# Expert layers on one core: the order of a pair's second matrix product and a later pair's first

## The reference, cut to what matters

```python
# layers 1 and 3 (F = 256): every token goes to one of 8 experts
h = jax.nn.gelu(xt @ W1[e], approximate=False) @ W2[e]
out = out + gate[:, None] * h
# layers 4 and 6 (H = 512): every token goes to its two best experts
h = jax.nn.gelu(jnp.einsum('bsd,dh->bsh', x, w1) + bb1, approximate=False)
y = jnp.einsum('bsh,hd->bsd', h, w2) + bb2
```

## Time and profile before

| | us |
|---|---|
| median of three runs | 1098.59 |
| the profiled execution | 1097.48 |
| its span, first to last instruction | 1095.7 |
| TensorE matmuls (PE) busy | 649.6 (59% of the span) |
| VectorE (DVE) busy | 763.3 (70%) |
| ScalarE (ACT) busy | 524.1 (48%) |
| GpSimd (POOL) busy | 544.0 (50%) |
| mean granted TensorE clock | 0.789 of full speed |

### The profile page before, as it was taken

The page is one execution under the profiler, slowest core; times in us unless marked ns, Lnnn a source line. Parts: engine busy times, 40 slices in busy tenths (PEclk is TensorE's granted clock), DMA queues, the critical chain, the costliest instruction groups (busy, mean ns, idle before and its releaser), DMA issues.

```text
span 1095.7 us, 18289 instructions
## 1 busy us (share of the span) xinstructions
PE 649.6 (59%) x5212; PEld 508.6 (46%) x5212; DVE 763.3 (70%) x2362; ACT 524.1 (48%) x1160; POOL 544.0 (50%) x562
## 2 busy tenths in 40 slices
PE   7014752579831467254698980387884469977810
PEld 7013541268720355253587870144563348765600
DVE  7884685989988457479376774499878737654742
ACT  3611333757560033052387881377874138854800
POOL 0006656587100463651767776554312467675575
PEclk9998975689955589555699996688886569986955
DMA  9602321000020133121233341111101024323232
GB/s 302 177 0 46 86 66 47 24 4 2 2 77 0 32 76 83 45 73 39 53 85 78 90 68 46 39 35 32 34 14 45 25 54 83 79 74 63 63 108 72
DMA packets 82494, 66.27 MB, mean 60 GB/s; under 512 B 10665, under 2 KB 74026, under 8 KB 82402
## 3 DMA queue, kind: packets, MB, share of 16 engines
q0 software_dynamic: 13728, 28.02, 11.7%
q1 hardware_dynamic: 68674, 37.09, 11.6%
HBM read 38.99 MB, written 26.08 MB: 59 GB/s over the span
## 4 chain that ended last, share of the span: by engine, by line
PE 28%; DVE 11%; issue 9%; POOL 6%; ACT 5%; another core or an unknown queue 4%; DMA 1%; DVEq 0%; ACTq 0%; POOLq 0%
PE bank L770 6%; POOL rt L1300 5%; PE bank L751 4%; PE bank L771 3%; PE bank L753 3%; PE bank L752 3%; ACT turned L826 1%; PE bank L735 1%; DVE turned L1123 1%; PE bank L1846 1%; PE bank L1810 1%; DVE x L1188 1%; ACT turned L831 1%; PE bank L1778 1%
## 5 line engine op out<-in xcount | busy, mean ns | idle before, releaser
L1277 POOL DMA_INDIRECT turned<-xrows_moe,token x234 | 253.0, 1081 | 313.1 <-DVE token L1043 203.1
L1300 POOL DMA_INDIRECT rt<-y_moe,slot_i x176 | 177.0, 1006 | 132.5 <-issue 53.1
L826 ACT ACTIVATE turned<-bank,b1T 128x256 f32<-128x256 f32 (+1 forms) x372 | 131.3, 444 | 93.5 <-remote 41.8
L751 PE MATMUL bank<-rt,w1h 128*128 128x128 bf16 (+1 forms) x528 | 138.2, 265 | 53.7 <-issue 24.9
L1123 DVE TENSOR_TENSOR turned<-turned 128x1024 bf16<-128x1024 f32 (+1 forms) x119 | 127.8, 1074 | 38.6 <-ACT turned L831 23.1
L752 PE MATMUL bank<-rt,w1h 128*128 128x128 bf16 (+1 forms) x528 | 137.1, 263 | 1.8 <-issue 1.7
L753 PE MATMUL bank<-rt,w1l 128*128 128x128 bf16 (+1 forms) x528 | 136.7, 262 | 1.0 <-issue 0.7
L770 PE MATMUL bank<-w_1s,turned 128*128 x624 | 120.1, 284 | 12.1 <-DVE turned L1123 6.1
L771 PE MATMUL bank<-w_1s,turned 128*128 x624 | 114.2, 226 | 2.6 <-issue 2.6
L817 ACT ACTIVATE turned<-bank 128x512 f32<-128x512 f32 x40 | 23.9, 598 | 161.1 <-issue 86.1
L1188 DVE SCALAR_TENSOR_TENSOR x<-rt,small,x 128x128 f32<-128x128 f32 x176 | 55.9, 347 | 58.6 <-DMA rt<-y_moe,slot_i 53.2
(11 more groups left out here) (334 smaller groups left out, 1750.5 us busy)
## 6 DMA issues: line engine op xcount, KB each, us to landing
y_moe<-arena SPq DMA_DIRECT2D x119, 128.0 KB
xrows_moe<-xn SPq DMA_DIRECT2D x8, 512.0 KB
turned<-xrows_moe,token POOLq DMA_INDIRECT x234
rt<-y_moe,slot_i POOLq DMA_INDIRECT x176
x<-in_x SPq DMA_DIRECT2D x4, 512.0 KB, 5.7
arena<-in_w SPq DMA_DIRECT2D x1, 2048.0 KB, 9.6
xn<-in_w SPq DMA_DIRECT2D x8, 256.0 KB, 4.8
xrows_moe<-arena SPq DMA_DIRECT2D x4, 512.0 KB
```

The lines of the kernel that those rows point to most:

```text
L751: nc.tensor.matmul(o, wh, xh_t, start=True, stop=False)
L826: last = nc.scalar.activation(s["h32"][:, t % 2, o:o + width], bank[1 + 2 * (t % 2) + u // 2][:, at:at + width], ACT.Gelu, bias=b1T[:, ds( ...
L1277: nc.gpsimd.indirect_dma_start(out=s["xs"][:, 2 * (t % BODY) + j], out_offset=None, in_=s["xdram"], in_offset=bass.IndirectOffsetOnAxis(ap ...
L1300: nc.gpsimd.indirect_dma_start(out=brought_to(s, n), out_offset=None, in_=s["ydram"][0:P * UNITS] if s["halves"] == 2 and at < PART else s ...
```

## The change

Within a step of TensorE's loop the second product of pair t is put ahead of the first product of pair t+2 (and of `known(t + 2)`). The turn of pair t+3 stays where it is. Nothing else changes: no instruction is added or taken away, and the loops of the other engines stay as they are.

```diff
@@ -789,10 +789,10 @@ def moe_tensor
             for t in range(pairs):
                 if t + 3 < pairs:
                     turn(t + 3)
+                down(t, experts.pop(t))
                 if t + 2 < pairs:
                     known(t + 2)
                     up(t + 2, experts[t + 2])
-                down(t, experts.pop(t))
```

## The result

The changed kernel takes **1142.28 us** (median of four runs, 1140.71 to 1145.06) against 1098.78 for the kernel before (four runs, 1097.95 to 1099.63): a ratio of 1.0401, 95% interval 1.0377 to 1.0425. It is 43.5 us slower. The forecast was 1130, the range 1112 to 1150.

What follows compares the result with a forecast made beforehand. TensorE was taken to bound the third layer, three engines close behind. Third layer 17.3, fourth 14.0, first two 0: 31.3 us on 1097.48 gives 1128.8, forecast 1130 as that execution stood 1.1 below the median; range 1112 to 1150.

Steps and rivals of the forecast that it cites:

- The circle: Last two layers: dependence over two pairs, ScalarE, `low`, second product, first product, ScalarE; 7.16 us, 3.58 a pair against 2.86.
- mixed pairs 12 to 20 of the fourth layer: 28.8 us before, 34.2 after by four circles of 8.56 us, +5.4 us.
- The signs in the profile: Third layer: L770 waits some 25 us for L1123, L751 hardly, chain alternates, PE about 80%; second layer within 3 us.
- The first and second layer: Their loops are not bound by the new dependence; gain and loss about cancel, 0 between -6.7 and +9.6 us.
- Rival A: Last two layers: ScalarE, `low` and hops fit PE's 3.1 us; 1092 us with first-layer gain (0.06), 1099 without (0.05).
- Rival B: Last two layers: waits of 0.72 us a pair lower TensorE's clock, 23 us on top, 1153 us; chance 0.07.
- waits are swallowed: Third layer: PE's 0.72 us of slack a pair absorbs the 8.6 us of other waits, giving +17.3 instead of +25.9.
- pairs 20 to 38 of the fourth layer: 81.9 us before, partly other waits; ends 0 and 12.7, taken as 6 x 0.68 for the mixed pairs, +4 us.
- Rival C: Last two layers: other waits add up, 8.6 and 8.7 us more, 1147 us; counted within the forecast's chance of 0.82.
- The third layer: Pairs 1 to 37: 111.6 us become 18 x 7.16 = 128.9, +17.3 us, ends +10.3 and +25.9.
- the fourth layer's start: Fourth layer from its start to pair 4: no change predicted, 0.
- the slack: Last two layers, pure pairs: TensorE's idle time waiting for `low`, 0.72 us a pair, expected to absorb other waits.

Runs made afterwards that it cites:

- small memset: Memset of 128x256 on VectorE ahead of each `low` in the last two layers: 1151.26 us (1.0390) on the new order, 1109.88 us (1.0028) on the old.

## Why the prediction was right, and where its sum was not

**The circle** is right, link by link: 7.16 us computed, 7.19 read in one turn, 7.20 the median. It was made of durations of the trace before, in an order that had never run. The experiments show that it binds: take half a second product out of the wait and most of the loss goes, lengthen a link by 0.20 or 0.47 us and the circle grows by as much. The first does nothing to the old order; the second was tried there with the small memset alone, and is not measurable. For the mixed pairs 12 to 20 of the fourth layer, 34.2 us came as computed, but this is partly luck: their circles are 8.3 to 9.1 us long and not 8.56 each, and the mean came out.

**The signs in the profile** came as described. L770 waits for L1123 (16.4 us of 19.7 in 110 us), L751 does not wait in the third layer, the chain alternates between engines, and the second layer's loop takes 59.0 us from its first to its last pair where it took 57.9. PE's share of the inner third layer is 83%, "about 80%" having been written.

**The first and second layer**, 0 between -6.7 and +9.6: measured +1.7 in the trace and +1.7 alone, the latter with an interval that takes in 0.

**Rival A**, not slower, falls with the circle: 4.4 us don't fit into 3.1. **Rival B**, the clock: the inner third layer has 0.98, so a wait of 0.70 us a pair did not lower it. Only the start of the layer was at the low level, after PE had idled 3.29 us for `low`; there the clock cost the 2.2 us shown above. No experiment turned on the clock alone.

**The mis-sized step is "waits are swallowed".** The span grew by 47.6, the forecast sum was 31.3, and 16.3 are missing. The sum took +4 for pairs 20 to 38 of the fourth layer, and +9.5 came: 5.5 of them. The third layer has 4.1, in the places shown, the fourth layer's start 2.0; the other 4.7 are small items of the table. Rival C, waits add up, had been priced at 8.6 and 8.7 us more. Pairs 20 to 38 take 54.7 us with the old order in the quietest of the experiments (the one with the new order up to t = 18), which is the rhythm alone, 12 x 2.86 + 6 x 3.4 (eight mixed pairs, 12 to 20, take 27.1 us there). So the profile before had 81.9 - 54.7 = 27.2 us of other waits there, and the profile after 91.4 - 68.6 = 22.8 beside its circles. By this estimate the slack swallowed 4.4 of 27.2. With the slowest of the kernels that have the old order there on the same chip, 60.3, and the measured 70.1 of the new order in place of 68.6, it is 21.6 before and 21.3 after, and nothing was swallowed. Either way, most of these waits stayed. ScalarE's timeline of that stretch shows where such waits are; one in the profile before, and then one in the profile after:

```profile
976.24 1.57 ACT L826 ACTIVATE turned<-bank,b1T 128x256 f32<-128x256 f32 x4 [5.38 <-remote]
```

```profile
1024.84 1.57 ACT L826 ACTIVATE turned<-bank,b1T 128x256 f32<-128x256 f32 x4 [10.33 <-remote]
```

These waits, five of 21.4 us in that stretch before and three of 22.3 after, are on the hop from the first product to ScalarE. My reading is that this hop is a link of the circle, so that what is late there is added to it, while the slack of 0.72 us is TensorE's and can only swallow a wait of TensorE's own. No run tried this by itself. In the third layer, where 8.6 us of other waits stood before, the time after is 4.1 over its circles, so there about half was swallowed. On the chip without "remote" waits the same stretch takes 70.1 us with the new order, close to the 68.6 of its circles, against 54.7 to 60.3 with the old one. So without such waits the circle is nearly all, as the prediction had it.

## What to carry to other kernels

Where engines execute in order and hand a tile round (ScalarE, VectorE, TensorE), look for the circle: follow the releases from one pair to the one that reuses the same queue place, add up the durations and hops of one trace, divide by the pairs it spans, and compare with the busiest engine's rhythm. Putting an instruction that waits ahead of one that doesn't pulls the producer of the wait into the circle. A wait that sits on a link of the circle adds to it, as the two long `low` did; one beside it can vanish in its slack. And before a step is moved on one engine, look at what is queued behind its consumer on the next.

## What was not expected of the hardware

**The same kernel, 1007 us on two chips and 1099 to 1107 us on the others.** On the slower ones other engines begin late after TensorE has finished, as the profile shows it. ScalarE's timeline at the start of the first layer's loop, in the profile before and then in the kernel with the new order from step 19 of the fourth layer on, which is the kernel before up to there and ran on a faster chip:

```profile
104.12 0.60 ACT L817 ACTIVATE turned<-bank 128x512 f32<-128x512 f32 x1 [8.83 <-remote]
```

```profile
95.91 0.60 ACT L821 ACTIVATE turned<-bank 128x512 f32<-128x512 f32 x1 [0.59 <-PE bank L753]
```

The list of waits of the profile before (us in total, times, longest us) has:

```profile
DVE arena L1138 <- remote: 43.7, 11, 11.4
ACT turned L826 <- remote: 41.8, 10, 10.8
```

In the profiles of the kernels on the faster chips no wait at all is put down to "remote". TensorE's own stream has gaps there too. In the timeline of PE after, within the second product that begins at 1016.01, nothing is waited for that the profile shows, and yet:

```profile
1020.35 0.22 PE L771 MATMUL bank<-w_1s,turned 128*128 x1 [0.94 <-issue]
```

The 16 matmuls take 4.4 us instead of 1.32. The first product for which ScalarE waits at this time ended near 1014.8, and ScalarE begins at 1024.84. All such stretches that I looked at lie where GpSimd issues gathers without a pause; but it does so on the faster chips as well, without the delay. So the gathers alone are not the cause. The mean granted clock differs too: 0.81 to 0.82 in the profiled executions on the two faster chips, 0.79 to 0.80 on the slower ones and in the profile before; whether that is a cause or follows from the waits, no run tells. What it is stays open.
